# Finding a cell's keys with one gather of two neighbouring runs instead of two gathers, in seven chunks under the node stage

## What is computed

```
n = 12500; x, out = features, features
for l in range(3):
    f1 = relu(x[row] @ nb_W[l] + nb_b[l])
    f2 = relu(x[col] @ self_W[l] + self_b[l])
    h = relu(concat([f1, f2]) @ att1_W[l] + att1_b[l])
    mask = clip(sigmoid(h @ att2_W[l] + att2_b[l]) * 1.5 - 0.45, 0, 1)
    d = clip((segment_sum(mask, row) + 1e-6) ** -0.5, 0, 10)
    x = segment_sum((mask * d[row] * d[col])[:, None] * x[col], row)
    out = out + x
x = layernorm(features + out)
x = layernorm(x + relu(segment_sum(x[col] * w[:, None], row) @ weight + bias))
```

## Time and profile before

| what | value |
| --- | --- |
| median of 3 runs | 9572.24 us (9570.25 to 9575.1) |
| the profiled execution | 9576.85 us |
| span of its profile | 9574.8 us, 756409 instructions |
| PE, DVE busy | 7886.7 us (82%), 7847.6 us (82%) |
| ACT, POOL busy | 3203.1 us (33%), 3663.7 us (38%) |
| end of the sort | 917 us |
| first one-hots of the edge stage | 1388 us |

### The profile page before, as it was taken

One profiled execution on the slowest core, in us unless ns is written; L12 is line 12 of the kernel. 1 busy time (PEld: TensorE's weight loads), 2 busy tenths in 40 slices (PEclk: granted clock), 3 DMA queues, 4 the chain that ended last, 5 costly groups with the idle time before them and its releaser, 6 DMA issues. The chain is left out here.

```text
span 9574.8 us, 756409 instructions
## 1 busy us (share of the span) xinstructions
PE 7886.7 (82%) x306604; PEld 7544.6 (79%) x306604; DVE 7847.6 (82%) x14021; ACT 3203.1 (33%) x6427; POOL 3663.7 (38%) x4224
## 2 busy tenths in 40 slices
PE   0012239999998999989999899989999899969998
PEld 0012128888887999989989899979999899969997
DVE  9999159999998888877777888877777888888887
ACT  0010016666666444410000344420000244434443
POOL 0001620000000888710000588820000388868885
PEclk9755559999998999999999999999999999989997
DMA  1000127777776666567777666657777666646664
GB/s 29 0 0 10 33 76 239 240 240 240 240 240 209 174 179 178 154 186 208 207 207 207 165 178 177 178 153 207 207 207 207 174 178 178 178 130 178 178 178 109
DMA packets 983691, 1593.41 MB, mean 166 GB/s; under 512 B 249800, under 2 KB 732940, under 8 KB 983216
## 3 DMA queue, kind: packets, MB, share of 16 engines
q1 hardware_dynamic: 954442, 1563.58, 56.0%
q0 software_dynamic: 29152, 28.55, 1.6%
HBM read 1308.68 MB, written 283.01 MB: 166 GB/s over the span
## 5 line engine op out<-in xcount | busy, mean ns | idle before, releaser
L1142 PE MATMUL bank<-tab,extra 128*64 128x64 bf16 x201684 | 3610.7, 197 | 355.9 <-issue 127.4
L1142 PEld LDWEIGHTS bank<-tab,extra 128*64 128x64 fp8e4 x201684 | 3488.8, 113 | 470.4 <-issue 443.2
L768 POOL TENSOR_TENSOR planes<-planes 128x448 f32<-128x448 f32 (+1 forms) x2744 | 2594.7, 948 | 516.7 <-DVE planes L1925 453.7
L977 ACT CAST bank<-planes 128x448 f32<-128x448 bf16 (+1 forms) x2744 | 1471.6, 545 | 1682.2 <-DVE planes L1918 1675.8
L1925 DVE TENSOR_TENSOR planes<-planes,bank 128x448 f32<-128x448 f32 (+1 forms) x2744 | 1711.7, 624 | 224.4 <-ACT bank L977 129.1
L1918 DVE TENSOR_TENSOR planes<-bank,mask_all 128x448 f32<-128x448 f32 (+2 forms) x2744 | 1668.7, 620 | 244.6 <-PE bank L1142 147.9
L1269 PE MATMUL bank<-planes,extra 128*64 128x192 bf16 x39200 | 1845.0, 248 | 19.5 <-POOL planes L768 8.3
L1269 PEld LDWEIGHTS bank<-planes,extra 128*64 128x64 fp8e4 x39200 | 1689.7, 108 | 64.2 <-issue 13.9
L698 POOL DMA_INDIRECT xg<-q_table,ixb x294 | 277.3, 943 | 3758.9 <-ACT ixb L901 2203.3
L1798 DVE SCALAR_TENSOR_TENSOR extra<-bank,a2w 128x448 f32<-128x448 f32 (+1 forms) x2058 | 1264.8, 630 | 448.2 <-PE bank L1165 411.2
L1165 PE MATMUL bank<-plb,extra 128*128 128x64 bf16 x44100 | 1523.5, 196 | 13.0 <-issue 2.8
(11 more groups left out here) (260 smaller groups left out, 4436.3 us busy)
## 6 DMA issues: line engine op xcount, KB each, us to landing
extra<-one_hots SPq DMA_DIRECT2D x1372, 352.0 KB, 3.1
extra<-one_hots SPq DMA_DIRECT2D x2156, 224.0 KB
extra<-one_hots SPq DMA_DIRECT2D x588, 208.0 KB, 2.8
one_hots<-extra SPq DMA_DIRECT2D x490, 224.0 KB, 3.9
one_hots<-extra SPq DMA_DIRECT2D x294, 352.0 KB, 4.4
work<-slot_rows_cols SPq DMA_DIRECT2D x196, 352.0 KB, 4.9
work<-slot_rows_cols SPq DMA_DIRECT2D x294, 224.0 KB, 4.9
work<-slot_rows_cols SPq DMA_DIRECT2D x98, 208.0 KB
```

Of the source, the lines that this page charges most:

```text
L768: nc.gpsimd.tensor_tensor(tiles(yrl[:, 2, a * C:b * C]), tiles(yrl[:, 1, a * C:b * C]), upper[:, 1, a:b, :], ALU.subtract).then_inc(low_re ...
L977: nc.scalar.copy(tiles(z_banks[g][:, 0:(b - a) * C]), upper[:, 0, a:b, :]).then_inc(high_ps, 1)
L1142: mm = pe.matmul(bank[half * S:(half + 1) * S, i * C:(i + 1) * C], oct_[:, k * P + half * S:k * P + (half + 1) * S], tab[:, at:at + C], st ...
```

## The change

- Before, the 64 keys from a cell's start on took two gathers: the run that holds the start, and then the keys. Now one gather brings the run and its right neighbour (128 keys, 512 bytes a row). The keys of the cell's 64 slots are chosen on VectorE: slot s takes the own run's key where that is not below the bound, and the neighbour's key at s otherwise. These are the same 64 keys in rotated order.
- `CHUNKS` are seven now (six of 14 bounds and one of 15), with two buffers (`runs`). GpSimd's gathers of chunk i wait for `runs_used` of chunk i-2, which `level3(i-2)` gives. The first chunk waits for round 2's first group alone, where it waited for two groups.
- `nodes_of` stands seven times, for one pair each, with `level3(i)` behind it and the fields of chunk i-1 (`fields`) behind that. The fields take one compare with the next cell's bound where they took a shift and a compare.
- `planes_of` moves ahead of the extra slots' fields; the copy into `colx` moves behind the slow path's setup; the extra slots' store and the last kind of `numbers` on SyncE move behind the other kinds.

```diff
-    CHUNKS = [range(c, min(c + 33, NC1)) for c in range(0, NC1, 33)]
+    CHUNKS = [range(c, c + 14 if c + 14 < NB else NC1) for c in range(0, NB, 14)]
...
-        slots = [mask_all[0:NB, 0:PER], mask_all[0:NB, PER:2 * PER], tab_f[0:NB, TS:TS + PER]]
+        RUNS = len(CHUNKS[-1]) * 2 * C
+        runs_at = 2 * 2 * CB * C + 2 * CB * P
+        runs = [tab_f[0:NB, TS:TS + RUNS], extra[0:NB, runs_at:runs_at + RUNS]]
...
-            for kind in KINDS:
+            for kind in KINDS[:-1]:
                 numbers(0, kind)
+            sp.wait_ge(lo_ready, len(LO_PARTS))
+            sp.dma_start(lo_d[:, MS // 4:TS // 4], lo8.bitcast(I32)[:, MS // 4:TS // 4]).then_inc(lo_x_out, 16)
+            sp.wait_ge(lo_x_out, 16)
+            numbers(0, LAST_MADE)
...
             for i, cs in enumerate(CHUNKS):
-                pool.wait_ge(run2_ready, 2 + i)
+                pool.wait_ge(run2_ready, cs[0] // 28 + 1 if cs[-1] < NB else len(ROUND2))
+                if i >= 2:
+                    pool.wait_ge(runs_used, i - 1)
                 for j, c in enumerate(cs):
-                    gather(slots[i][:, j * C:(j + 1) * C], sorted_d, run2_i[:, c:c + 1], level3_in[i])
-            for i, cs in enumerate(CHUNKS):
-                pool.wait_ge(start_ready, i + 1)
-                for c in cs:
-                    if c < NB:
-                        gather(keys[:, c * S:(c + 1) * S], sorted_flat, start_i[:, c:c + 1], keys_in[i])
+                    gather(runs[i % 2][:, j * 2 * C:(j + 1) * 2 * C], sorted_d, run2_i[:, c:c + 1], level3_in[i])
             pool.wait_ge(pos_ready, 1)
...
             def level3(i):
...
+                both = runs[i % 2][:, 0:n * 2 * C].rearrange("p (c h s) -> p c h s", h=2, s=C)
+                own, next_run = both[:, :, 0, :], both[:, :, 1, :]
...
+                dve.wait_ge(level3_in[i], 16 * n)
+                st.done(v.tensor_tensor(low, own, thr[:, at].unsqueeze(2).to_broadcast([NB, n, C]), ALU.is_lt))
+                st.wait(dve)
+                st.done(v.tensor_reduce(cnt[:, at], low, AX_X, ALU.add))
+                st.done(v.tensor_tensor(to, low[:, 0:kept, :], next_run[:, 0:kept, :], ALU.mult))
+                st.wait(dve)
                 st.done(v.scalar_tensor_tensor(start[:, at], run2[:, at], float(C), cnt[:, at], ALU.mult, ALU.add))
+                st.done(v.tensor_tensor(to, to, own[:, 0:kept, :], ALU.max))
                 st.wait(dve)
+                dve.sem_inc(runs_used, 1)
+
+            def fields(i):
...
+                st.done(v.tensor_tensor(by_run(invalid[:, a:b]), by_run(keys[:, a:b]),
+                                        thr[:, ca + 1:cb + 1].unsqueeze(2).to_broadcast([NB, cb - ca, S]), ALU.is_ge))
+                st.done(v.tensor_scalar(lo, keys_i[:, a:b], PB, P - 1, sh_r, band))
                 st.wait(dve)
+                st.done(v.scalar_tensor_tensor(lo8[:, a:b], invalid[:, a:b], float(P), lo, ALU.mult, ALU.add))
                 st.wait(dve)
+                st.done(v.tensor_scalar(lo, keys_i[:, a:b], P - 1, None, band))
+                st.wait(dve)
+                st.done(v.scalar_tensor_tensor(lo8[:, TS + a:TS + b], invalid[:, a:b], float(P), lo, ALU.mult, ALU.add))
+                st.wait(dve)
+                dve.sem_inc(lo_ready, 1)
...
-            nodes_of(0, True, range(0, 2))
-            level3(0)
-            nodes_of(0, True, range(2, 3))
-            level3(1)
-            nodes_of(0, True, range(3, 4))
-            level3(2)
+            for i in range(len(CHUNKS)):
+                nodes_of(0, True, range(i, i + 1))
+                level3(i)
+                if i:
+                    fields(i - 1)
...
-            nodes_of(0, True, range(4, NCH // 2))
+            fields(len(CHUNKS) - 1)
...
+            planes_of(0, "first")
+            dve.wait_ge(shifted_in, XP * 16)
...
             dve.sem_inc(lo_ready, 1)
-            planes_of(0, "first")
```

More of the change, by code:

```diff
@@ L92, in gnn_kernel @@
     NC1 = NB + 1
-    CHUNKS = [range(c, min(c + 33, NC1)) for c in range(0, NC1, 33)]
+    CHUNKS = [range(c, c + 14 if c + 14 < NB else NC1) for c in range(0, NB, 14)]
     ROUND2 = [range(c, min(c + 28, NC1)) for c in range(0, NC1, 28)]
     LO_PARTS = [(cs[0] * S, min(cs[-1] + 1, NB) * S) for cs in CHUNKS] + [(MS, TS)]
-    LO_STORES = 2 * len(CHUNKS) + 1
+    LO_STORES = 2 * len(CHUNKS)
+    assert len(CHUNKS) == NCH // 2 and all(cs[0] // 28 == min(cs[-1], NB - 1) // 28 for cs in CHUNKS)
     LANES = max(n for n in range(1, P + 1) if E % n == 0)
@@ L157, in gnn_kernel @@
         thr = thr_i.bitcast(F32)
-        thr_hi = take(NC1, I32)
         iota_c = take(NC1, I32)
@@ L164, in gnn_kernel @@
         run2, run2_i = take(NC1), take(NC1, I32)
-        start, start_i = take(NC1), take(NC1, I32)
+        start = take(NC1)
         n_f, n_i = take(NB), take(NB, I32)
@@ L195, in gnn_kernel @@
         invalid = mask_all[0:NB, :].bitcast(U8)[:, TS + MS:TS + 2 * MS]
-        assert (TS + 2 * MS) // 4 <= NB * TT and 2 * PER <= NB * TT
+        assert (TS + 2 * MS) // 4 <= NB * TT
         rb = work[:].bitcast(U8)[:, 0:TS + MS]
@@ L287, in gnn_kernel @@
         round2_used = sem("round2_used")
-        level3_in = [sem(f"level3_in{i}") for i in range(3)]
+        level3_in = [sem(f"level3_in{i}") for i in range(len(CHUNKS))]
+        runs_used = sem("runs_used")
         run2_ready = sem("run2_ready")
-        start_ready = sem("start_ready")
-        keys_in = [sem(f"keys_in{i}") for i in range(4)]
+        shifted_in = sem("shifted_in")
         pos_ready = sem("pos_ready")
@@ L1568, in level3 @@
             def level3(i):
-                cs = CHUNKS[i]
-                dve.wait_ge(level3_in[i], 16 * len(cs))
-                at = below(slots[i], cs)
+                c0, n = CHUNKS[i][0], len(CHUNKS[i])
+                kept = min(n, NB - c0)
+                at = slice(c0, c0 + n)
+                both = runs[i % 2][:, 0:n * 2 * C].rearrange("p (c h s) -> p c h s", h=2, s=C)
+                own, next_run = both[:, :, 0, :], both[:, :, 1, :]
+                low = cmp2[:, 0:n * C].rearrange("p (c s) -> p c s", s=C)
@@ L1572, in level3 @@
+                to = keys[:, c0 * S:(c0 + kept) * S].rearrange("p (c s) -> p c s", s=S)
+                dve.wait_ge(level3_in[i], 16 * n)
[4 more added lines that the diff above has]
+                st.wait(dve)
                 st.done(v.scalar_tensor_tensor(start[:, at], run2[:, at], float(C), cnt[:, at], ALU.mult, ALU.add))
+                st.done(v.tensor_tensor(to, to, own[:, 0:kept, :], ALU.max))
@@ L1759, in _ @@
                     dve.sem_inc(xsteps, X_STEPS - xt.n)
+            dve.wait_ge(xcolT_ps, 1)
+            st.done(v.tensor_copy(colx[:].rearrange("p (r t) -> p t r", t=XT),
+                                  banks[2][:, 0:XT * NB].rearrange("p (t r) -> p t r", r=NB)))
+            st.wait(dve)
+            dve.sem_inc(colx_ready, 1)
             dve.wait_ge(lo_out, LO_STORES * 16)
+            dve.wait_ge(lo_x_out, 16)
             def scaled_table(k, rows, factor):
```

49 lines of the change are left out of this document (13 added, 36 removed).

## The result

| | before | after |
| --- | --- | --- |
| median | 9573.67 us (9570.25 to 9577.85, 4 runs) | 9430.69 us (9430.21 to 9433.18, 4 runs) |
| ratio, 95% interval | | 0.985 [0.9838, 0.9862] |
| span of the profile | 9574.8 us | 9428.1 us |
| round 2's end to the first one-hots | 425.7 us | 286.7 us (962.7 to 1249.4) |
| gathers of the search's chunks | 197 | 99 |

The kernel is 143 us faster, where 130 was forecast. The stretch that the sum went over gives 139.0 of them. In the new kernel L698 is L706, L1551 is L1554, round 2's compare L1493 is L1496, its cast L1502 is L1505, ScalarE's L872 is L877, TensorE's L1098 is L1103 and the first one-hots' L1814 is L1817.

A forecast was written before the change was run, and what follows sets the result against it. It took the bound as a DVE chain of node pairs, where POOL's gathers delay PE's matmul completions. Terms summed to 295.0 us against 425.7, 130.7 us less than 9576.85, so 9442 us forecast with the median's offset (range 9378 to 9500).

The forecast's parts named there:

- round 2's end (962.7) to the end of pair 1: First node pair, partly under the first burst of 28 gathers: taken to end at 1000 us, 37.3 us.
- pairs 2 to 6: Node pairs with a 17.9 us burst each: 10 us free, the rest held up, 26 us each, 130 us in all.
- pair 7: Last node pair, with no burst of gathers beside it: 17.5 us.
- between the pairs, up to the positions: DVE's work between node pairs: seven `level3` at 4.5 us and six `fields` at 4.4, 57.9 us.
- positions to the first one-hots: Behind the last node pair: positions, last fields, `ctl`, `planes_of`, extra slots' fields, setup and `colx`, 52.3 us.
- Gathers: The search's gathers on POOL: 197 become 99, 128 keys take as long as 64, 125 us of bursts less.
- wide gathers dear: Rival on POOL: gathers of 128 keys take twice as long, bursts 35.8 us; 9568 us, no change; chance 0.03.
- The "remote" waits: Sign in DVE's waits before L1554 that end by nothing local: down from 196.5 to some 50 to 60 us.
- First passes of each piece of the loop: Rival: first passes through each copy of DVE's node loop are slow, 50.2 us each; 9608 us, slower; chance 0.05.
- Whole bursts lost: Rival: node pairs are held up for the entire burst, second to sixth at 35.4 us; 9499 us; chance 0.20.
- Short bursts cost nothing: Rival: bursts of 17.9 us hardly hold up node pairs, second to sixth take 17.5 us; 9380 us; chance 0.17.

The follow-up runs named there:

- one_ahead: The changed kernel, but GpSimd gathers one chunk ahead instead of two, so the first burst is 14 gathers; 9418.6 us, ratio 0.984.
- twice: The changed kernel with a spare gather of 98 rows of 64 keys behind every gather of chunks 2 to 6; 9509.15 us, ratio 0.9939.
- halves: The changed kernel, but from chunk 2 on a chunk's second seven gathers wait for the middle of the node pair; 9397.51 us, ratio 0.9817.
- late_start: The changed kernel, but the first chunk's gathers wait for round 2's second group again; 9427.11 us, ratio 0.9851.

## Why the prediction was right

**The view that carried it** was the comparison of pairs with and without gathers beside them, read with the earlier trace rows. It gave a size (a pair under a burst loses what lies behind its first 10 us) that held roughly in the change, one_ahead and twice, where burst and pair start within some 4 us of each other, and not in halves. Term by term:

| term | forecast | measured |
| --- | --- | --- |
| round 2's end (962.7) to the end of pair 1 | 37.3 | 40.0 |
| pairs 2 to 6 | 130 | 115.7 |
| pair 7 | 17.5 | 17.1 |
| between the pairs, up to the positions | 57.9 | 60.4 |
| positions to the first one-hots | 52.3 | 53.5 |
| sum | 295.0 | 286.7 |

- *Gathers*: right. 969 ns at 128 keys, 1.28 us apart; "wide gathers dear" falls.
- *First pair*: right within 3 us, which is partly luck. I let round 2 lose the time but started pair 1 at 989 or, with the end of 1000 that I took, at 982.5. Round 2 ended at 985.2, since the groups' completions were late from the third on, 15 us into the burst; pair 1 behind it lay free. In late_start the pair loses 17.8 us and round 2 nothing, where in the change round 2 ended 22.5 us later than before.
- *Pairs 2 to 6*: mechanism right, size off by 14.3 us. "10 us run freely, the remaining 8 nearly nothing" was too harsh: the pairs lose 5 to 7.5 us and not 8.5. The prediction's suspicion that a burst with a start of some 4 us on the pair costs less is not borne out: the third pair has that start and still takes 24.0 us, and one_ahead's pairs with it take 23 to 24.
- *The "remote" waits*: the sign-post was wrong (13.3 us, not 50 to 60). The earlier trace rows has one line of one engine, 196.5 of 288.2 us. Which engine's wait carries the name depends on which completion happens to be due; now it is more often the one that ScalarE's L877 waits for (40.1 us). The sum of 81.9 us over the three lines is no measure either, since they stand partly behind one another. Pair lengths are.
- *Between and behind the pairs*: right. A `level3` took 4.6 us against 4.5, a `fields` 4.7 against 4.4 (an integer shift of this size takes 0.62 us, not 0.55). SyncE's stores stayed hidden. The prediction held that nothing behind the first one-hots changes. The two profiles are 141.3 us apart at the start of layer 2's node stage and 146.7 at the end, so 7.7 us came in behind the stretch; where they come from wasn't looked into.

The sum came out 8.3 us too high: 14.7 us too much for pairs 2 to 7 hide 6.4 too little elsewhere.

**The rivals.** *First passes of each piece of the loop* falls by the first and the seventh window: both are first passes through a copy of their own, and take 16.8 and 17.1 us. *Whole bursts lost* falls by 22 to 24.5 us against 35. *Short bursts cost nothing* is wrong on the first kind of chip, and its sum, 233.5 us, is to within a microsecond what the change takes on the other kind (233.9). The Trainium skill (SBUF — State Buffer, "SBUF: two separate sides") says that DMA and compute can't slow each other. The second kind of chip agrees with that here (17.2 us with 12 gathers beside the third pair), and the first doesn't (23.9 us). The section speaks of ports, and what comes late here is the signal that a matmul is done; no run shows whether a port has part in it. What I hadn't asked is what the kernel *before* would take in that case: there it loses its hold-up too, and the gain is 86 us and not 190. The chance I gave that case was for a cheap short burst, not for a chip that has no hold-up.

## What to carry to other kernels

When one engine's completions arrive late, put equal pieces of work side by side by what ran beside them, and change that neighbour's rhythm before its amount: the same fourteen gathers cost nothing with a pause in the middle of the pair, where in one go beside it they cost 6 us, and a wait on a semaphore that is due anyway is all it takes. Then look in the trace at what the rhythm became; here it wasn't the one that had been planned. A gather of 128 keys took GpSimd no longer than one of 64 (969 ns each). And profile both kernels on a second chip before a stall goes into a cost model: here some 61 of 139 us differed between one set of runs and the next.

## What the runs showed of the hardware

- Two kinds of chips, or of sets of runs. Three sets had the kernel before at 9565 to 9574 us, two at 9178 to 9184. On the first kind, completions of TensorE's f32 matmuls come late when matmuls run beside a row of indirect gathers 1.28 us apart. In the change the third group of round 2 was due at 952.7, some 10 us into the burst, and was taken at 957.3. Under 99 gathers a pair's 50 matmuls took 125 us, an estimate of 2.5 us each. Nothing was late beside the pairs of halves, with a pause of 5.4 to 7.1 us in each, or beside gathers 1.87 us apart. On the second kind nothing of it shows in a row of 98 gathers over 128 us. The cause inside the chip stays open.
- The kinds also differ where no search is. The same 1500 us of the trace, all in the first layer's edge stage (which starts 117 us earlier on the second), kernel before, first on the one and then on the other:

```profile
1400.00:2900.00 1500.00, 1418.62 (x47514) 1308.16 (x47516) 1348.24 (x2268) 993.11 (x1749) 82.04 (x87) 0.90 0.73 239
```

```profile
1400.00:2900.00 1500.00, 1394.76 (x50183) 1294.53 (x50181) 1428.86 (x2439) 1057.66 (x1859) 103.37 (x112) 0.96 0.78 252
```

The granted clock is 0.90 and 0.96, and the second gets through 6% more matmuls. Of the 397 us between the two spans the stretch of the search makes 114; the rest is outside it, and no experiment here was on it.
